# A decoder layer on one core: score and sum matmuls moved next to each other in TensorE's order

## The chip, the core and the metric

The kernel runs on one core of a Trainium2 chip. The metric is the device time of one execution in microseconds; less is better. The core's engines run their own instruction streams and wait for each other by semaphores: TensorE (PE in the profile, with its weight loads as PEld), VectorE (DVE), ScalarE (ACT), GpSimd (POOL), and SyncE, which here issues DMAs (SPq is its queue).

## What is computed

32 sequences of 128 tokens by 256 features go through one pre-normalised decoder layer in fp32. Cut to what matters:

```python
x = x + linear_attention(layernorm(x))      # 16 heads of 16: q, k = elu(.)+1; causal sums
x = x + cross_attention(layernorm(x), ctx)  # 16 heads of 16: softmax(q k^T / 4) v
x = x + ffn(layernorm(x))                   # 256 -> 1024 (gated) -> 1024 -> 1024 -> 256
# causal linear attention, per head:
num = einsum('bhsd,bhsde->bhse', q, cumsum(k[..., :, None] * v[..., None, :]))
out = num / (einsum('bhsd,bhsd->bhs', q, cumsum(k)) + 1e-6)
# ffn: ternary weights w with a scale s per output column
h = silu(tlin(h, w1)) * tlin(h, w2); h = gelu(tlin(h, h1)); h = gelu(tlin(h, h2)); out = tlin(h, w3)
```

The kernel computes the causal sums as masked scores: k q^T for each head, everything above the diagonal set to zero, times v with a column of ones beside it, whose sum is the denominator.

## The kernel before

**Work and tiling.** Attention goes by groups g = 0 to 15 of two sequences (b = 0, 1). The feed-forward part goes by turns f = 0 to 7 of 512 tokens, that is of two groups. A turn is the steps `gate` (L918), `hidden` (L933) and `w3` (L948): each step is a run of 4 matmuls of 128x128 weights by 512 columns. A turn of the feed-forward part has 16 gate steps, 64 hidden steps and 8 w3 steps, and the attention steps of later groups are strewn among them.

**Steps that use a part of the array.** The helper `scores` (L816) makes for one sequence the scores of 16 heads: contraction over 32 rows, four row quarters of the array at a time (`tile_position=(32 * r, 0)`), into four banks. It serves three steps: `lin_scores` (operands `qf,kz`), `max` (`xkz,xqf`; only to find the row maxima) and `x_scores` (`xqf,xkz`, behind four small bf16 matmuls at L809 that add the shift). The profile counts 32 matmul records for one such step. The helper `add_up` (L789) multiplies scores by values: outputs of 32 columns, four column quarters of the array (`tile_position=(0, 32 * j)`), 16 records for two tiles of scores (a "pair"). Its steps are `lin_sums` (`att_l,v`) and `x_sums` (`att_x,xv`), four pairs per group: pairs 0 and 1 for the first sequence, 2 and 3 for the second. All other matmuls and transposes use the whole array.

**What happens around them.** Linear attention: `lin_scores` b, then for each of its four tiles n `lin_copy` on ScalarE (L533, PSUM to `att_l`) and on GpSimd (L469, times the causal mask); `lin_sums` pair; `lin_out` on ScalarE (L500, PSUM to `sums`); `lin_turn` on TensorE (L798, transposes), then VectorE divides. Cross attention: `x_scores` b, `x_exp` on ScalarE (L563), `x_sums`, `x_out` (L500), `x_turn` (L798). `att_l` and `att_x` are rings of `NL, NX = 4, 4` tiles. `bias` on GpSimd (L475) adds a bias to the residual input `xb`. `load_ctx` on SyncE (L421) loads the context of the next group once its last readers on TensorE are through, for `xv` (L775) and `xk`; `ring` on SyncE (L388) loads the next weights into one of 4 slots once the matmuls that read the slot are through. ScalarE's gelu (L593, L599) releases the banks of `hidden`.

**What sets the order.** A table of numbers. `steady(name, n, engine=t, ...)` puts a step of group g into each named engine's list at nominal time begin(g) + stretch * t (2.2 from group 4 on), and `put` does so for the feed-forward steps. Each list is sorted by nominal time, and every engine executes its list in that order, blocking at a wait. The nominal time sets the order and nothing else. TensorE's list then goes through a planner that gives each step its PSUM bank(s), the ones that are nominally free first, and that puts a step back if none is free; `wait_pbank` makes the step wait for the last reader of that bank.

## Time and profile before

| | |
|---|---|
| time, median of 3 runs | 1188.05 us (1187.08 to 1190.3) |
| time of the profiled execution | 1188.87 us |
| its span in the profile | 1187.1 us |
| TensorE busy | 1139.9 us, 96% of the span |
| ScalarE, VectorE, GpSimd busy | 51%, 50%, 29% |
| chain that ended last, TensorE's share | 91% |

The span runs from the first to the last instruction; 1.8 us of the time lie outside it. The share of a busy TensorE counts a matmul from its start to its end, so a start that comes late behind another matmul's end is not seen as idle. The chain follows the end of the program back, instruction by instruction, to what released each.

### The profile page before, as it was taken

To read this page: it belongs to the slowest core of one execution; us is meant where nothing else is said; L and a number is where in the kernel's file an instruction comes from. 1 tells how busy PE (TensorE), PEld (TensorE's weight loads), DVE (VectorE), ACT (ScalarE), POOL (GpSimd) and SP (SyncE) were. 2 spreads that over 40 slices of the span, in tenths; PEclk is the share of its full clock that TensorE was granted. 3 is DMA by queue.
4 is the path that set the end of the run, shared out by engine and by line. 5 is a ranking of instruction groups with operands and counts; after the bars stand their busy time and mean duration, and the time that the engine had idled before them with its cause. 6 is when DMAs were issued, how large, how long until landed. Compare 5 with 4: busy or idle time off the path is not lost.

```text
span 1187.1 us, 24494 instructions
## 1 busy us (share of the span) xinstructions
PE 1139.9 (96%) x9666; PEld 902.2 (76%) x9666; DVE 588.0 (50%) x1381; ACT 601.3 (51%) x1078; POOL 339.8 (29%) x378
## 2 busy tenths in 40 slices
PE   4777999999999999999999999999999999999997
PEld 3665878778787877878777787877877787787886
DVE  2545653348344564535555465445744456443511
ACT  2345464635538365474645546374563736545432
POOL 3334260132503244042430415213250233400300
PEclk8899999999999999999999999999999999999999
DMA  3143554234423343325333253322442335333742
GB/s 112 63 151 91 152 187 160 90 110 157 144 76 108 133 161 121 97 93 175 109 122 105 81 182 120 128 94 92 170 144 84 106 127 169 106 106 116 245 149 73
DMA packets 62500, 148.58 MB, mean 125 GB/s; under 512 B 5936, under 2 KB 21424, under 8 KB 62384
## 3 DMA queue, kind: packets, MB, share of 16 engines
q1 hardware_dynamic: 58928, 135.44, 34.3%
q10 hardware_dynamic: 3456, 11.54, 3.2%
q8 instruction: 80, 1.31, 0.4%
q14 instruction: 36, 0.29, 0.1%
HBM read 130.17 MB, written 28.31 MB: 134 GB/s over the span
## 4 chain that ended last, share of the span: by engine, by line
PE 91%; DMA 3%; DVE 2%; issue 1%; ACT 1%; POOL 1%; SPq 0%; ACTq 0%; POOLq 0%; DVEq 0%
PE bank L933 41%; PE bank L918 10%; PE bank L766 9%; PE bank L816 8%; PE bank L789 5%; PE bank L775 5%; PE bank L948 5%; PE bank L798 2%; PE bank L758 2%; PE bank L874 2%; DMA ctxs<-in_ctxT 2%; PE bank L809 1%; DMA weight_ring<-weights_scratch 1%; POOL att_l L469 1%; PE bank L891 1%
## 5 line engine op out<-in xcount | busy, mean ns | idle before, releaser
L933 PE MATMUL bank<-hidden_b,weight_ring 128*128 128x512 f32 x1024 | 272.0, 407 | 0.0
L933 PE MATMUL bank<-hidden_a,weight_ring 128*128 128x512 f32 x1024 | 270.4, 406 | 0.0
L469 POOL TENSOR_TENSOR att_l<-att_l,cst 128x512 f32<-128x512 f32 x128 | 165.1, 1301 | 345.1 <-ACT att_l L533 344.7
L933 PEld LDWEIGHTS bank<-hidden_a,weight_ring 128*128 128x128 f32 x1024 | 185.4, 188 | 43.7 <-issue 6.9
L933 PEld LDWEIGHTS bank<-hidden_b,weight_ring 128*128 128x128 f32 x1024 | 184.2, 188 | 44.4 <-issue 6.7
L593 ACT ACTIVATE hidden_full<-bank,columns_sb 128x512 f32<-128x512 f32 x128 | 88.2, 689 | 197.9 <-PE bank L933 196.9
L918 PE MATMUL bank<-hidden_b,weight_ring 128*128 128x512 f32 x512 | 143.3, 414 | 0.7 <-DVE mx L689 0.6
L480 POOL TENSOR_TENSOR hidden_a<-hidden_full,hidden_a 128x512 fp32r<-128x512 f32 x64 | 82.2, 1290 | 171.7 <-ACT hidden_a L588 171.7
L629 DVE TENSOR_SCALAR denom<-bank 128x16 f32<-128x16 f32 x64 | 11.1, 174 | 203.6 <-PE bank L798 203.5
L918 PEld LDWEIGHTS bank<-hidden_b,weight_ring 128*128 128x128 f32 x512 | 91.7, 188 | 19.5 <-DVE mx L689 1.3
L728 DVE TENSOR_TENSOR hidden_b<-hidden_full,hidden_b 128x512 fp32r<-128x512 f32 x64 | 44.4, 695 | 116.9 <-ACT hidden_b L599 116.9
L451 POOL TENSOR_TENSOR ve<-mv,eps 128x1 f32<-128x1 f32 (+1 forms) x80 | 23.4, 292 | 256.3 <-DVE mv L608 256.3
L689 DVE TENSOR_REDUCE mx<-bank 128x4 f32<-128x512 f32 x128 | 83.8, 682 | 17.6 <-PE bank L816 17.6
L728 DVE TENSOR_TENSOR hidden_a<-hidden_full,hidden_a 128x512 fp32r<-128x512 f32 x64 | 44.4, 694 | 86.3 <-ACT hidden_a L599 86.0
L533 ACT ACTIVATE att_l<-bank 128x512 f32<-128x512 f32 x128 | 74.8, 606 | 18.1 <-PE bank L816 18.1
L563 ACT ACTIVATE att_x<-bank 128x512 f32<-128x512 f32 x128 | 66.4, 603 | 21.7 <-PE bank L816 21.6
L500 ACT ACTIVATE sums<-bank 128x256 f32<-128x256 f32 x128 | 47.2, 391 | 50.7 <-PE bank L789 50.3
L948 PE MATMUL bank<-hidden_a,weight_ring 128*128 128x512 f32 x256 | 68.0, 406 | 0.7 <-DMA weight_ring<-weights_scratch 0.7
L720 DVE SCALAR_TENSOR_TENSOR hidden_full<-hidden_full,bank 128x512 f32<-128x512 f32 x64 | 43.7, 683 | 29.2 <-ACT hidden_full L583 29.1
L583 ACT ACTIVATE hidden_full<-bank,s1h 128x512 f32<-128x512 f32 x64 | 44.0, 687 | 23.9 <-PE bank L918 21.1
L723 DVE SCALAR_TENSOR_TENSOR hidden_full<-bank,s,hidden_full 128x512 f32<-128x512 f32 x64 | 48.1, 751 | 14.1 <-PE bank L918 12.3
L948 PEld LDWEIGHTS bank<-hidden_a,weight_ring 128*128 128x128 f32 x256 | 46.9, 188 | 10.6 <-DMA weight_ring<-weights_scratch 1.5
(98 smaller groups left out, 1682.7 us busy)
## 6 DMA issues: line engine op xcount, KB each, us to landing
weight_ring<-weights_scratch SPq DMA_DIRECT2D x160, 512.0 KB, 3.4
weights_scratch<-in_h ACTq DMA_DIRECT2D x16, 512.0 KB, 4.5
xn3T_scratch<-hidden_b SPq DMA_DIRECT2D x16, 512.0 KB, 5.9
weight_ring<-weights_scratch SPq DMA_DIRECT2D x32, 256.0 KB, 2.9
weight_bits<-in_h SPq DMA_DIRECT2D x32, 256.0 KB, 3.7
x_in<-in_x SPq DMA_DIRECT2D x16, 256.0 KB, 4.0
xb<-in_x SPq DMA_DIRECT2D x16, 256.0 KB, 5.1
ctxs<-in_ctxT SPq DMA_DIRECT2D x16, 256.0 KB, 3.8
```

The costliest lines, as they stand in the source:

```text
L469: eng.tensor_tensor(slot, slot, causal.rearrange("p (o s) -> p o s", o=1).broadcast_to([P, 4, S]), ALU.mult)\
L480: eng.tensor_tensor(HA[:, 1, n, :], full[:, n % NFULL, :], HA[:, 0, n, :].bitcast(F32), ALU.subtract)\
L533: eng.activation(att_l[:, (NU * g + n) % NL, :, :], pbank("lin_scores", g, n)[:, :].rearrange("p (j s) -> p j s", j=4), ACT.Copy)\
L563: eng.activation(att_x[:, (NU * g + n) % NX, :, :], pbank("x_scores", g, n)[:, :].rearrange("p (j s) -> p j s", j=4), ACT.Exp, scale=SCALE ...
L593: eng.activation(full[:, (KH + n) % NFULL, :], pbank("hidden", g, n)[:, :], ACT.Gelu, scale=sc).then_inc(h_full, 1)
L689: eng.tensor_reduce(mx[:, b, 4 * r:4 * r + 4], pbank("max", g, n)[:, :].rearrange("p (j t) -> p j t", j=4), AX.X, ALU.max).then_inc(max_do ...
L728: eng.tensor_tensor(dst[:, 1, m, :], full[:, (KH + n) % NFULL, :], dst[:, 0, m, :].bitcast(F32), ALU.subtract)\
L766: mm = eng.matmul(pbank(step, g)[:, m * T:(m + 1) * T], w[:, c, m * P:(m + 1) * P], src[:, c, :], start=(c == 0), stop=(c == C - 1))
L816: mm = eng.matmul(pbank(step, g, 4 * b + r)[:, j * S:(j + 1) * S], stationary(rows, e, m, b), moving(rows, e, m, b), start=not shifted, st ...
L918: mm = eng.matmul(pbank(step, g, n)[:, :], ring[:, n // 4, at_:at_ + P], HB[:, part, kk, :], start=(kk == 0 and part == 0), stop=(kk == C ...
L933: mm = eng.matmul(pbank(step, g, n)[:, :], ring[:, slot, kk * P:(kk + 1) * P], src[:, part, kk, :], start=(kk == 0 and part == 0), stop=(k ...
L948: mm = eng.matmul(pbank(step, g, c)[:, :], ring[:, slot, kk % 4 * P:(kk % 4 + 1) * P], HA[:, part, kk, :], start=(kk == 0 and part == 0), ...
```

## The change

In the table the two pairs of one sequence get one nominal time (from group 4 on; earlier groups keep two), and a new pass goes over TensorE's sorted list: where of two steps among `lin_scores`, `max`, `x_scores`, `lin_sums`, `x_sums` only `gate`, `hidden` or `w3` steps stand between and the nominal times lie less than `JOIN = 1.59` apart, the earlier one is moved to stand directly in front of the later. Both pairs of a sequence now share one bank (`u = 2 * m + pair % 2`), which is waited for once and read by one ScalarE copy of 128x512 in place of two of 128x256. The rings `att_l` and `att_x` get 8 tiles. Some forty numbers of the table change besides, among them the places of `bias`, `lin_copy`, `load_ctx`, `ring` and of the tests of the weights' low bits (`load_bits`, `low_bits`). What the matmuls compute does not change.

```diff
@@ -34,6 +34,7 @@
     QUARTER = TURN / 88
     EARLY = ((0, 1.15), (28, 1), (66, 1.3), (110, 1.91))
     STRETCH = 2.2
+    JOIN = 1.59
...
-        steady("k", tensor=-5.41, scalar=-4.5, vector=-3.74)
+        steady("q", tensor=-8, scalar=-6.79, vector=-5.41)
+        steady("k", tensor=-4.93, scalar=-4.02, vector=-3.26)
...
+        steady("v", tensor=-4.17, vector=-0.29)
+        steady("load_xb", sync=0.96)
+        steady("bias", gpsimd=7.57)
+        steady("load_ctx", sync=8.45)
         for b in range(GB):
-            steady("lin_scores", b, tensor=-0.25 + 4.6 * b)
+            steady("lin_scores", b, tensor=-0.73 + 4.6 * b)
         for n in range(NU):
-            u = 0.32 + 1.35 * n
-            steady("lin_copy", n, scalar=u + 0.02, gpsimd=u - 1.61)
-            if n % 2:
-                steady("lin_sums", n // 2, tensor=u + 1.7)
-                steady("lin_out", n // 2, scalar=u + 2.98)
+            u = 0.32 + 1.07 * n
+            steady("lin_copy", n, scalar=u + 0.02, gpsimd=u - 0.41)
         for b in range(GB):
+            for h in range(2):
+                if early:
+                    u = 3.37 + 5.4 * b + 2.64 * h
+                else:
+                    u = 4.37 + 6.89 * b + 0.01 * h
+                steady("lin_sums", 2 * b + h, tensor=u + 0)
+            steady("lin_out", b, scalar=u + 0.41)
             u = 7.2 + 5.4 * b
-            steady("lin_turn", b, tensor=u - 0.33, vector=u - 0.03)
...
-            steady("project", b, tensor=u + 3.54, vector=u + 4.38, gpsimd=u + 3.93)
+            steady("project", b, tensor=u + 3.8, vector=u + 4.38, gpsimd=u + 5.74)
...
-            w = 30.6 + 3 * b + 0.15 * u
+            w = 30.6 + 3.62 * b + 0.15 * u
             steady("x_exp", n, scalar=w - 0.09)
-            if u % 2:
-                steady("x_sums", n // 2, tensor=w + 0.71)
-                steady("x_out", n // 2, scalar=w + 1.54)
         for b in range(GB):
+            for h in range(2):
+                if early:
+                    u = 31.75 + 3.07 * b + 0.3 * h
+                else:
+                    u = 31.42 + 3.72 * b + 0.01 * h
+                steady("x_sums", 2 * b + h, tensor=u - 0.1)
+            steady("x_out", b, scalar=u + 0.83)
             u = 27.6 + 3.21 * b
-            steady("shift", b, vector=u - 0.34, tensor=u + 0.29, scalar=u + 0.9)
+            steady("shift", b, vector=u - 0.87, tensor=u - 0.42, scalar=u + 0.9)
             u = 34.4 + 7.19 * b
-            steady("x_turn", b, tensor=u - 0.09, vector=u - 0.4, gpsimd=u + 0.29)
-            steady("ln3", b, vector=u + 3.82)
+            steady("x_turn", b, tensor=u - 1.47, vector=u - 0.36, gpsimd=u + 1.64)
+            steady("ln3", b, vector=u + 3.63)
 
 
...
             elif j < RING:
-                u = (-14.33, -1.3, -6.15, 0.27)[j]
+                u = (-8.49, -0.79, -6.15, 0.01)[j]
...
-            put(at, "ring", f, j, sync=u - 5.45)
+            put(at, "ring", f, j, sync=u + 0.35)
...
-            u = 193.16 + 110.03 * i + 18 * j
-            put(0, "load_bits", i, j, sync=u - 0.79)
-            put(0, "low_bits", i, j, vector=u + 14.31)
+            u = 185.4 + 116.28 * i + 18.39 * j
+            put(0, "load_bits", i, j, sync=u - 1.28)
+            put(0, "low_bits", i, j, vector=u + 11.62)
...
+    order = program["tensor"]
+    for i in reversed(range(len(order))):
+        if order[i][1] in ("lin_scores", "max", "x_scores", "lin_sums", "x_sums"):
+            j = i - 1
+            while j > 0 and order[j][1] in ("gate", "hidden", "w3"):
+                j -= 1
+            if j >= 0 and order[j][1] in ("lin_scores", "max", "x_scores", "lin_sums", "x_sums") and order[i][0] - order[j][0] < JOIN:
+                order.insert(i - 1, (order[i][0], *order.pop(j)[1:]))
...
-            NL, NX = 4, 4
+            NL, NX = 8, 8
...
-                    "lin_sums": ("scalar", "lin_out", sums_done[0], NU // 2), "x_sums": ("scalar", "x_out", sums_done[1], NU // 2),
+                    "lin_sums": ("scalar", "lin_out", sums_done[0], GB), "x_sums": ("scalar", "x_out", sums_done[1], GB),
...
                 t, step, g, n = pending.pop()
                 if step in ("hidden", "w3"):
                     uses = [n // 4] if n % 4 == 0 else []
+                elif step in ("lin_sums", "x_sums"):
+                    uses = [n // 2] if n % 2 == 0 else []
                 elif step in ("lin_scores", "max", "x_scores"):
...
-                def sums_out(which, step, g, pair):
-
-                    eng.wait_ge(summed[which], 4 * g + pair + 1)
-                    if pair % 2 == 0:
-                        wait_count(eng, sums_turned[which], GB * g + pair // 2)
-                    eng.activation(sums[:, which, :, :].rearrange("p (c q) s -> p q c s", q=2)[:, pair % 2],
-                                   pbank(step, g, pair)[:, 0:2 * S].rearrange("p (c s) -> p c s", c=C), ACT.Copy)\
+                def sums_out(which, step, g, b):
+
+                    eng.wait_ge(summed[which], 4 * g + 2 * b + 2)
+                    wait_count(eng, sums_turned[which], GB * g + b)
+                    eng.activation(sums[:, which, :, :], pbank(step, g, b)[:, :].rearrange("p (u s) -> p u s", u=4), ACT.Copy)\
                        .then_inc(sums_done[which], 1)
...
                     b = pair // 2
                     eng.wait_ge(ready, NU * g + 2 * pair + 2)
-                    wait_pbank(eng, step, g, pair)
+                    if pair % 2 == 0:
+                        wait_pbank(eng, step, g, b)
                     for m in range(C):
                         for n in (2 * pair, 2 * pair + 1):
                             for e in range(2):
                                 j = 2 * (n % 2) + e
-                                mm = eng.matmul(pbank(step, g, pair)[32 * j:32 * j + 32, m * S:(m + 1) * S],
+                                u = 2 * m + pair % 2
+                                mm = eng.matmul(pbank(step, g, b)[32 * j:32 * j + 32, u * S:(u + 1) * S],
                                                 vt[:, b, 8 * m + 2 * (n % 4) + e, :], att[:, (NU * g + n) % slots, 2 * m + e, :],
                                                 start=True, stop=True, tile_position=(0, 32 * j))
                     mm.then_inc(summed[which], 1)
 
                 def turn_sums(step, which, g, b):
-                    eng.wait_ge(sums_done[which], 4 * g + 2 * b + 2)
+                    eng.wait_ge(sums_done[which], GB * g + b + 1)
                     wait_pbank(eng, step, g, b)
```

**TensorE's order.** The first place is group 8's first sequence between the second cross-attention scores of group 7 (L809 and L816 `xqf,xkz`) and the sums of group 8, before:

```order
L809 MATMUL bank<-shiftT,onesb 128x512 x4
L816 MATMUL bank<-xqf,xkz 128x128 x16
L933 MATMUL bank<-hidden_b,weight_ring 128x512 x12
L798 MATMUL bank<-cst,sums 128x128 x4
L789 MATMUL bank<-att_x,xv 32x128 x8
L789 MATMUL bank<-att_l,v 32x128 x8
L789 MATMUL bank<-att_x,xv 32x128 x8
L933 MATMUL bank<-hidden_b,weight_ring 128x512 x4
L816 MATMUL bank<-qf,kz 128x128 x16
L933 MATMUL bank<-hidden_b,weight_ring 128x512 x12
L789 MATMUL bank<-att_l,v 32x128 x8
```

The same place of the changed kernel (its L812 is the sums, L839 the scores, L956 `hidden`):

```order
L832 MATMUL bank<-shiftT,onesb 128x512 x4
L839 MATMUL bank<-xqf,xkz 128x128 x16
L956 MATMUL bank<-hidden_b,weight_ring 128x512 x4
L821 MATMUL bank<-cst,sums 128x128 x4
L956 MATMUL bank<-hidden_b,weight_ring 128x512 x12
L839 MATMUL bank<-qf,kz 128x128 x16
L812 MATMUL bank<-att_x,xv 32x128 x16
L812 MATMUL bank<-att_l,v 32x128 x16
L956 MATMUL bank<-hidden_b,weight_ring 128x512 x16
```

The linear scores of the second sequence, both pairs of `x_sums` and both pairs of `lin_sums` now stand in one run; the second pair of `lin_sums` (last row before) has moved ahead of twelve `hidden` matmuls.

**SyncE's order.** The second place is the load of the context of group 5 (`ctxs`) among the weight loads, before:

```order
L388 DMA weight_ring<-weights_scratch 128x1024 x3
L397 DMA weight_bits<-in_h 128x512
L388 DMA weight_ring<-weights_scratch 128x1024
L421 DMA ctxs<-in_ctxT 128x2x256
L371 DMA x_in<-in_x 128x2x256
```

And of the changed kernel:

```order
L411 DMA weight_ring<-weights_scratch 128x1024
L420 DMA weight_bits<-in_h 128x512
L411 DMA weight_ring<-weights_scratch 128x1024 x2
L444 DMA ctxs<-in_ctxT 128x2x256
L394 DMA x_in<-in_x 128x2x256
```

The context load now goes out one weight load earlier: of the four weight loads that stood ahead of it here three are left.

**GpSimd's order.** The third place is the first group: the masks of its eight tiles (`att_l`) and the bias on `xb`, before:

```order
L469 TENSOR_TENSOR att_l<-att_l,cst 128x512 x6
L475 TENSOR_TENSOR xb<-xb,bob 128x512
L469 TENSOR_TENSOR att_l<-att_l,cst 128x512 x2
```

And of the changed kernel:

```order
L492 TENSOR_TENSOR att_l<-att_l,cst 128x512 x8
L498 TENSOR_TENSOR xb<-xb,bob 128x512
```

The bias has moved behind the last two masks; so it has in the later groups.

## Rows read from the trace of the kernel before

**Rows 1.** The page: span, and busy time of each engine.

```profile
span 1187.1 us, 24494 instructions
...
PE 1139.9 (96%) x9666; PEld 902.2 (76%) x9666; DVE 588.0 (50%) x1381; ACT 601.3 (51%) x1078; POOL 339.8 (29%) x378
```

**Rows 2.** Windows of the span: PE, PEld, DVE, ACT, POOL busy, PE clock, DMA.

```profile
0.00:121.50 121.50, 85.33 (x1033) 66.30 (x1034) 53.62 (x164) 46.41 (x99) 47.09 (x63) 0.92 0.33 102
...
545.70:687.10 141.40, 141.24 (x1210) 111.73 (x1209) 74.94 (x175) 76.78 (x136) 42.50 (x46) 1.00 0.36 122
...
1111.30:1187.10 75.80, 69.00 (x306) 56.75 (x304) 18.99 (x30) 24.49 (x39) 6.56 (x6) 0.99 0.39 128
```

**Rows 3.** Chain that ended last, 504 to 540: start us, us, what.

```profile
517.37 1.45 PE bank L789 x48
518.81 1.14 PE bank L933 x4
...
524.02 0.57 PE bank L789 x16
...
538.83 0.92 PE bank L933 x4
```

**Rows 4.** TensorE's timeline, 61 to 63.6: start us, us, instruction.

```profile
61.23 1.07 PE L816 MATMUL bank<-xqf,xkz 32*128 32x128 f32 x32
62.23 0.65 PE L789 MATMUL bank<-att_l,v 128*32 128x128 f32 x16
```

**Rows 5.** TensorE's timeline, 504 to 520.

```profile
505.04 1.06 PE L816 MATMUL bank<-xqf,xkz 32*128 32x128 f32 x32
506.03 2.11 PE L933 MATMUL bank<-hidden_b,weight_ring 128*128 128x512 f32 x8
...
512.67 0.39 PE L809 MATMUL bank<-shiftT,onesb 2*128 2x512 bf16 x4
```

**Rows 6.** All engines' waits: engine, line, waited for: us, times, longest.

```profile
PE bank L775 <- DMA ctxs<-in_ctxT: 2.1, 3, 1.2
```

**Rows 7.** The queues' timeline (SyncE), 303 to 320.

```profile
307.23 7.47 SPq L388 DMA_DIRECT2D weight_ring<-weights_scratch  x3
...
319.10 0.32 SPq L388 DMA_DIRECT2D weight_ring<-weights_scratch  x1
319.52 0.38 SPq L421 DMA_DIRECT2D ctxs<-in_ctxT  x1
```

**Rows 8.** The chain, 318 to 332.

```profile
319.52 5.57 DMA ctxs<-in_ctxT
...
325.13 1.99 PE bank L775 x8
```

**Rows 9.** The chain, 27 to 36 and 107 to 120.

```profile
30.70 1.23 POOL xb L475
...
34.43 1.08 PE bank L789 x16
...
113.33 1.23 POOL xb L475
```

**Rows 10.** ScalarE's groups: line, operation, shapes, count, busy, mean ns.

```profile
L533 ACT ACTIVATE att_l<-bank 128x512 f32<-128x512 f32 x128 | 74.8, 606 | 18.1 <-PE bank L816 18.1
...
L500 ACT ACTIVATE sums<-bank 128x256 f32<-128x256 f32 x128 | 47.2, 391 | 50.7 <-PE bank L789 50.3
```

**Rows 11.** ScalarE's timeline, 504 to 521.

```profile
510.14 0.68 ACT L599 ACTIVATE hidden_a<-bank,columns_sb 128x512 fp32r<-128x512 f32 x1
...
514.15 2.07 ACT L563 ACTIVATE att_x<-bank 128x512 f32<-128x512 f32 x4
...
519.44 0.61 ACT L533 ACTIVATE att_l<-bank 128x512 f32<-128x512 f32 x1
```

**Rows 12.** GpSimd's timeline, 510 to 526.

```profile
520.12 1.39 POOL L469 TENSOR_TENSOR att_l<-att_l,cst 128x512 f32<-128x512 f32 x1 [2.07 <-ACT att_l L533]
```

More of the change, by code:

```diff
@@ L48, in decoder_layer_program @@
         at, stretch = begin(g)
+        early = g < len(EARLY)
         def steady(step, n=0, **slots):
             put(at, step, g, n, stretch, **slots)
-        steady("load_x", sync=-21.29)
-        steady("ln1_stats", vector=-14.57, gpsimd=-14.11)
-        steady("ln1", vector=-10.72)
+        steady("load_x", sync=-21.65)
+        steady("ln1_stats", vector=-18.26, gpsimd=-16.9)
+        steady("ln1", vector=-11.07)
         steady("ln1T", tensor=-9.02, scalar=-8.85)
-        steady("q", tensor=-8.4, scalar=-6.79, vector=-5.28)
@@ L58, in decoder_layer_program @@
-        steady("k", tensor=-5.41, scalar=-4.5, vector=-3.74)
+        steady("q", tensor=-8, scalar=-6.79, vector=-5.41)
+        steady("k", tensor=-4.93, scalar=-4.02, vector=-3.26)
         steady("k_heads", vector=-3.21)
-        steady("v", tensor=-4.49, vector=-1.75)
-        steady("load_xb", sync=1.83)
-        steady("bias", gpsimd=6.19)
-        steady("load_ctx", sync=9.29)
+        steady("v", tensor=-4.17, vector=-0.29)
+        steady("load_xb", sync=0.96)
+        steady("bias", gpsimd=7.57)
@@ L73, in decoder_layer_program @@
+        for b in range(GB):
+            for h in range(2):
[5 more added lines that the diff above has]
+            steady("lin_out", b, scalar=u + 0.41)
             u = 7.2 + 5.4 * b
-            steady("lin_turn", b, tensor=u - 0.33, vector=u - 0.03)
+            steady("lin_turn", b, tensor=u - 0.33, vector=u + 0.45)
             steady("o_turn", b, tensor=u + 1.41, scalar=u + 2)
-            steady("project", b, tensor=u + 3.54, vector=u + 4.38, gpsimd=u + 3.93)
@@ L77, in decoder_layer_program @@
-            steady("ln2", b, vector=u + 6.1)
-        steady("ln2T", tensor=18.75, scalar=19.89)
-        steady("xq", tensor=20.91, scalar=22.32)
-        steady("xk", tensor=16.95, scalar=17.71)
-        steady("xv", tensor=12.26, scalar=18.48)
+            steady("project", b, tensor=u + 3.8, vector=u + 4.38, gpsimd=u + 5.74)
+            steady("ln2", b, vector=u + 6.15)
+        steady("ln2T", tensor=18.94, scalar=19.14)
+        steady("xq", tensor=20.91, scalar=22.03)
+        steady("xk", tensor=16.95, scalar=21.19)
@@ L82, in decoder_layer_program @@
+        steady("xv", tensor=12.26, scalar=17.81)
         for b in range(GB):
@@ L119, in decoder_layer_program @@
         for p in range(2):
-            put(at, "xn3T", 2 * f + p, tensor=-10.32 + 2.6 * p, scalar=-8.56 + 2.6 * p, vector=-7.36 + 2.6 * p)
+            put(at, "xn3T", 2 * f + p, tensor=-9.46 + 2.6 * p, scalar=-5.61 + 2.6 * p, vector=-6.5 + 2.6 * p)
             put(at, "x2T", 2 * f + p, tensor=10.79 + 1.5 * p, scalar=12.21 + 1.5 * p)
-        put(at, "keep_xn", f, sync=5.63)
-        put(at, "keep_x2", f, sync=19.84)
+        put(at, "keep_xn", f, sync=10.53)
+        put(at, "keep_x2", f, sync=15.41)
         for m in range(KH):
@@ L129, in decoder_layer_program @@
             put(at, "gated", f, m, vector=u + 2 * QUARTER + 0.54)
-            put(at, "gate_round", f, m, scalar=u + 2 * QUARTER + 5.26)
-            put(at, "gate_rest", f, m, gpsimd=u + 2 * QUARTER + 3.78)
+            put(at, "gate_round", f, m, scalar=u + 2 * QUARTER + 5.16)
+            put(at, "gate_rest", f, m, gpsimd=u + 2 * QUARTER + 4.74)
         for n in range(2 * KH):
@@ L147, in decoder_layer_program @@
             if f == 0 and j < RING:
-                u = -32.71 + j
+                u = -33.84 + j
             elif j < RING:
-                u = (-14.33, -1.3, -6.15, 0.27)[j]
+                u = (-8.49, -0.79, -6.15, 0.01)[j]
             elif j < 2 * RING:
```

## Prediction

> **What bounds the kernel now.** I read the page first: TensorE is busy for 1139.9 of 1187.1 us, ScalarE for 51%, VectorE for 50%, GpSimd for 29% [rows 1]. The windows show where the rest lies: in the first 121.5 us TensorE works for 85.33, after that it is as good as never idle (141.24 of 141.40 us in one turn of the feed-forward part, the last 75.8 us apart) [rows 2]. So between 121.5 and about 1111 us whatever shortens TensorE's stream shortens the kernel, and whatever shortens another engine's does nothing. Busy is not the same as useful, though, and for that the chain of the end is the view, since it gives to each run of matmuls the time by which it holds up the next. Four `hidden` matmuls cost 0.92 us behind a whole-array step, and 1.14 behind sums, though they are the same instructions [rows 3]. One pair of sums by itself costs 0.57, three pairs in a run 1.45 [rows 3]: a further pair costs (1.45 - 0.57) / 2 = 0.44, the first 0.13 more. So a run of steps on quarters of the array pays 0.13 us to begin (if it begins with sums) and 0.21 to end (1.13 less 0.92). The change takes away such beginnings and ends.
>
> **Fewer runs.** I counted the runs in the two orders of TensorE: 169 before, 116 after. From group 3 on, a group had eleven (two `max`, two `x_scores`, two `lin_scores`, five of sums) and has seven. Up to the first `gate` step there are 17 and 16, so nearly the whole saving, 52 runs, falls where TensorE bounds. At 0.21 each that is 52 x 0.21 = 10.9 us. Places at which sums begin (behind the whole array or behind scores) are 85 before and 61 after, 15 and 16 of them up to the first `gate`, so 70 and 45 in the part that counts: 25 x 0.13 = 3.25 us. That scores to sums costs the same 0.13 as whole array to sums is the one price that has to be argued, since there are 27 such places (scores, then sums) where there were 4, and 10 the other way where there were 4. One of the four shows scores starting at 61.23 and the sums behind them at 62.23, 1.00 apart; scores with `hidden` behind them have 505.04 and 506.03, 0.99 apart [rows 4, 5]. Going from row quarters to column quarters holds the array up just as going to the whole array does, so it isn't free. It could be cheaper at the other end only if nothing were paid in the run's first sums: then I lose nothing of the sum and gain 29 x 0.13 = 3.8 us. It could cost an end and a beginning, 0.34: then 29 x 0.21 = 6.1 us go back. I take 0.13, by the row. Sum: 10.9 + 3.25 = 14.2 us.
>
> The Trainium skill, in TensorEngine Tiling (Array Packing), section Tiling Modes, says that changing the tiling mode, not just the tile, drains TensorE. By that rule scores next to sums save only one of two drains, and only sums next to sums, or scores next to scores, save both. The trace agrees, with its 1.00 and 0.99 us; with a free change the sum would be the 3.8 us larger.
>
> **Context loads.** TensorE waits three times, 2.1 us in all, for the context that `xv` reads [rows 6]. One of them: the load goes out at 319.52, takes 5.57 us, and `xv` starts at 325.13 [rows 7, 8]. It goes out then because the weight load ahead of it in SyncE's queue waited until 319.10 for its slot [rows 7]. Now the load stands in front of that weight load, behind one that had gone out by 307.23 + 7.47 = 314.70 [rows 7]. That is over 4 us earlier against a longest wait of 1.2, so I take the whole of it: 2.1 us. The weight load itself has three other slots' worth of matmuls as cover.
>
> **The first 121.5 us.** Here chains of all engines bound, and the bias on GpSimd is in them twice, 1.23 us each, between masks that the last sums of a sequence wait for [rows 9]. It now follows the masks: -2.5 us, unless at the first place other work of ScalarE takes over (the sums started at 34.43 [rows 9]). Against this each exposed copy of a sequence's sums is one of 128x512 where the last of two of 128x256 was waited for. ScalarE takes 606 ns for a 128x512 copy and 391 for a 128x256 one [rows 10]: 0.2 us more, at some five places on the chain, +1.0. Together 1.5 us. The order of a dozen other steps changes here too, and TensorE's clock is at its lower level for part of this stretch (mean 0.92 [rows 2]), so this term may be 2.5 us off either way.
>
> **New waits where TensorE bounds.** A wait that recurs in each of 13 groups costs 13 times itself, so I looked at three, around 512 us.
> (1) The second `lin_sums` pair moves ahead of twelve matmuls. It needs mask 3, which ended at 520.12 + 1.39 = 521.51, as its ScalarE copy ran only at 519.44 [rows 11, 12]. By the chain's prices the pair now stands at about 520.6: second `x_scores` at 512.5 (512.67 less one end), 1.2 for it, four `hidden` 1.1, `x_turn` 0.4, twelve `hidden` 2.8, scores 1.1, two `x_sums` pairs 1.0, one `lin_sums` pair 0.4. Unmoved, the mask would cost 0.9. But the copy is now put right behind the four exponentials, which end at 514.15 + 2.07 = 516.22 [rows 11] and may come half a microsecond later: copy to about 517.4, mask to 518.8. 1.8 us to spare.
> (2) The second `x_scores` needs the bank of the first `x_sums`, now freed by one copy. Before it on ScalarE stand the gelu that ends at 510.14 + 0.68 = 510.82 [rows 11] and two 128x512 copies; copies follow each other at 0.5 us, so the bank is free at 510.82 + 3 x 0.5 + 0.1 = 512.4. TensorE gets there at 512.5 [rows 5]. Nothing to spare: between 0 and 0.5 us in the six or so groups that lie like this.
> (3) Eight tiles in each ring take away the waits of ScalarE's copies for sums; that only helps.
> I put 1.0 us for all of this, with 0 and 4 as its ends.
>
> **Sum.** 14.2 + 2.1 + 1.5 - 1.0 = 16.8 us off the profiled 1188.9: 1172.1. The median of the runs is 0.8 us below that execution, so 1171.3; I say 1171.5. With the terms' ends (changes of mode 3.8 less or 6.1 more, start-up 2.5, waits 1 and 3) this case reaches from 1166 to 1178; chance 0.72.
>
> **Rivals.**
> *Change of mode dear.* Scores to sums costs an end and a beginning: 6.1 us more, 1177.5. Against it stand the 1.00 and 0.99 us; for it, that the end of a run on the whole array is paid partly in its first matmuls, which these two starts don't show. Chance 0.08.
> *Packed runs starve.* Three microseconds of scores and sums in one run fill banks faster than ScalarE, at 606 ns a bank [rows 10], reads them, and (1) or (2) turns into 0.4 to 0.9 us in each of 13 groups: 5 to 12 us back, 1176.5 to 1183.5. For it: no slack at (2), and 0.9 us at (1) if the copy slips. Against: ScalarE is idle for half of its time. Chance 0.10.
> The page just named says, under PSUM Bottleneck, that tiling speeds up TensorE but not the reading of its results, which may become the limit; that speaks for this rival, and the 606 ns are its measure here.
> *Slower.* In ScalarE's queue the copy of the linear sums stands ahead of the next gelu and waits for the whole run of scores and sums; if the gelu comes late, its bank and then `hidden` do. The run ends at about 521.0, the copies of the sums by 522.3, and the gelu's matmuls end at about the same time, so I see no delay. It decides from 16.8 / 13 = 1.3 us a group on: with 2 us a group, 26 in all, it would be 1171.5 + 26 = 1197.5. Chance 0.04.
> *No change.* The runs get fewer but TensorE was waiting on something else under cover of long matmuls. About 1188. The prices 0.21 and 0.13 come from a stretch in which TensorE doesn't wait, so I give this 0.03.
> *More.* A change of mode half paid, and start-up shorter by 4: 1163 to 1166. Chance 0.03.
>
> **How the numbers follow.** The predicted time is that of the first case. The range 1163.5 to 1181 holds it, the dear change, two thirds of the starving case and most of the last: about 0.88 by these chances; I keep it so because the start-up is ordered anew in more places than I could price. Repeated runs differ by 0.3%, 3.6 us; faster than 1184.5 are all cases but the last two signs, slower and no change: 0.93. Within 0.3% 0.03, slower 0.04.
>
> **What would show it.** In the changed kernel's chain: sums behind scores in one piece with a single 1.1 us `hidden` group behind them; sums of two pairs 0.88 to 1.0; a turn of the feed-forward part (141.4 us now) at about 139.2, since two groups save 2.2; no wait for `ctxs`; no `xb` on the chain before the first gate. It is wrong if a turn takes 140 or more, or if waits of sums for `att_l` or of scores for `sums` recur with each group.

## The result, and the profile of the changed kernel

The changed kernel takes 1172.53 us (median of 4 runs, 1168.11 to 1174.07) where the kernel before takes 1188.68 (1187.08 to 1190.3) beside it: ratio 0.9858, 95% interval 0.9827 to 0.9889. Its profiled execution took 1171.52 us, with a span of 1169.7. The prediction was 1171.5.

The page of the changed kernel, to be held against [rows 1]:

```profile
span 1169.7 us, 24358 instructions
...
PE 1127.3 (96%) x9666; PEld 907.8 (78%) x9666; DVE 600.8 (51%) x1381; ACT 593.3 (51%) x1014; POOL 341.8 (29%) x378
```

The same number of matmuls keeps TensorE busy for 12.6 us less, and ScalarE issues 64 instructions less (64 copies of sums in place of 128). The windows, now for the stretch up to the first `gate`, one turn, and the end (to be held against [rows 2]):

```profile
0.00:117.30 117.30, 86.00 (x1028) 67.12 (x1029) 53.33 (x161) 45.43 (x89) 47.18 (x63) 0.88 0.33 105
545.50:684.50 139.00, 138.76 (x1209) 112.34 (x1208) 75.53 (x175) 75.69 (x129) 42.96 (x46) 1.00 0.37 122
1100.00:1169.70 69.70, 63.21 (x281) 51.92 (x279) 14.50 (x25) 20.70 (x33) 1.29 (x1) 0.99 0.36 122
```

The start-up has got shorter although its mean clock is lower, 0.88: up to the first `gate` TensorE ran 27.3 us at its lower clock, in the profile of the kernel before 20.5. The turn takes 139.0 us with as many matmuls as the 141.4 of before. From the starts of the `gate` batches in both traces: up to the first 119.82 and 116.97 us (-2.85); first to second 147.08 and 144.35 (-2.73); second to seventh, five turns or ten groups, 708.85 and 698.57 (-10.28); seventh to eighth -1.38; from there to the end -0.16. Together the 17.4 us by which the spans differ.

The chain of the end, around the place that the prediction looked at (start us, us, what):

```profile
500.38 1.10 PE bank L839 x32
501.48 1.01 PE bank L812 x32
502.49 2.04 PE bank L956 x8
...
510.07 1.10 PE bank L839 x32
511.17 1.88 PE bank L812 x64
513.05 1.16 PE bank L956 x4
...
516.23 1.44 DVE weight_bits L759
...
518.29 0.67 DVE xn L632
...
519.36 0.43 DVE o L657
...
519.84 0.44 PE bank L889 x2
```

L839 is the helper of the scores here, L812 that of the sums, L956 `hidden`, L889 `o_turn`. The upper rows show what was meant to happen: scores, then two or four pairs of sums (1.01 and 1.88 us) in one piece, and one slow group of `hidden` (1.16) behind it. The lower rows show what nobody had asked for: the chain leaves TensorE and goes through VectorE, whose test of the weights' low bits and whose normalization `xn` (step `ln3`) stand ahead of the division `o` that `o_turn` waits for. TensorE's waits say how often (us, times, longest):

```profile
PE bank L889 <- DVE o L657: 7.0, 12, 1.3
```

Before, the same wait was 3.6 us in 4 places. A wait for `ctxs` is no longer among TensorE's.

To see where ten groups' time goes I took, for each change from one kind of matmul to another in the five turns, the time from the last start of the one to the second start of the other, and called a wait what it exceeded the usual time of that kind by (usual over all the kernels of this document). Before: 704.45 us of regular stream and 4.4 of waits (2.85 of them three waits for `ctxs`). After: 693.05 and 5.5 (4.65 of them `o_turn`). So the regular stream gave 11.40 us in ten groups, and the waits took 1.1 back.

### The profile page after: what moved, and what is told of

It is laid out like the page before. It is cut to its first block, busy times and chain, and to the rows that moved or that the text cites. A ratio compares the mean times of both kernels' runs of the same rounds, so it can differ in the third digit from the quotient of the medians.

```text
span 1169.7 us, 24358 instructions
## 1 busy us (share of the span) xinstructions
PE 1127.3 (96%) x9666; PEld 907.8 (78%) x9666; DVE 600.8 (51%) x1381; ACT 593.3 (51%) x1014; POOL 341.8 (29%) x378
## 4 chain that ended last, share of the span: by engine, by line
PE 89%; DVE 4%; ACT 3%; issue 2%; POOL 1%; DMA 0%; SPq 0%; ACTq 0%; POOLq 0%; DVEq 0%
PE bank L956 37%; PE bank L941 10%; PE bank L787 9%; PE bank L839 8%; PE bank L971 5%; PE bank L796 5%; PE bank L812 5%; PE bank L897 3%; PE bank L779 2%; PE bank L821 2%; DVE xn L632 1%; PE bank L832 1%; PE bank L889 1%; ACT L614 1%; PE bank L914 1%
## 5 line engine op out<-in xcount | busy, mean ns | idle before, releaser
L956 PE MATMUL bank<-hidden_b,weight_ring 128*128 128x512 f32 x1024 | 264.7, 403 | 0.0
L956 PE MATMUL bank<-hidden_a,weight_ring 128*128 128x512 f32 x1024 | 264.0, 403 | 0.0
L956 PEld LDWEIGHTS bank<-hidden_a,weight_ring 128*128 128x128 f32 x1024 | 186.0, 188 | 40.7 <-issue 4.4
L956 PEld LDWEIGHTS bank<-hidden_b,weight_ring 128*128 128x128 f32 x1024 | 184.9, 188 | 41.3 <-issue 3.8
L941 PE MATMUL bank<-hidden_b,weight_ring 128*128 128x512 f32 x512 | 140.4, 411 | 0.0
L971 PE MATMUL bank<-hidden_a,weight_ring 128*128 128x512 f32 x256 | 67.8, 406 | 0.0
L522 ACT ACTIVATE sums<-bank 128x512 f32<-128x512 f32 x64 | 37.3, 603 | 41.2 <-PE bank L812 41.2
```

What stands on the lines that cost most here:

```text
L941: mm = eng.matmul(pbank(step, g, n)[:, :], ring[:, n // 4, at_:at_ + P], HB[:, part, kk, :], start=(kk == 0 and part == 0), stop=(kk == C ...
L956: mm = eng.matmul(pbank(step, g, n)[:, :], ring[:, slot, kk * P:(kk + 1) * P], src[:, part, kk, :], start=(kk == 0 and part == 0), stop=(k ...
L971: mm = eng.matmul(pbank(step, g, c)[:, :], ring[:, slot, kk % 4 * P:(kk % 4 + 1) * P], HA[:, part, kk, :], start=(kk == 0 and part == 0), ...
```

## Experiments

Times are medians; the kernel before stood at 1189.12, 1188.61 and 1189.46 us in the three sets.

**1. The pairs apart again.** The changed kernel with no joining pass and, for every group, the numbers of the early ones, so that pairs and scores stand alone again (167 runs on quarters of the array; 116 in the changed kernel). One bank for both pairs, the rings and all other numbers stay.

```diff
-    JOIN = 1.59
+    JOIN = 0
...
-                    u = 4.37 + 6.89 * b + 0.01 * h
+                    u = 3.37 + 5.4 * b + 2.64 * h
...
-                    u = 31.42 + 3.72 * b + 0.01 * h
+                    u = 31.75 + 3.07 * b + 0.3 * h
```

> The changed kernel with the two pairs of a sequence apart again in the table (the numbers of the early groups for all) and without the pass that joins; one bank, 8 tiles and all other new numbers stay. 167 runs in TensorE's order instead of 116, and sums begin at 98 places instead of 61. Theory (switching is paid for by TensorE): 51 x 0.21 + 37 x 0.13 = 15.5 us slower than the changed kernel, so about 1187 to 1188 us. Rival (the other numbers of the table made the gain): within 4 us of the changed kernel, 1170 to 1176.

1187.17 us, ratio 0.9989 (0.9978 to 1.0): nearly the whole gain is gone. The five turns take 712.30 us, 13.7 more than in the changed kernel: 705.48 of regular stream, 12.4 more, and 6.8 of waits, 1.3 more, now mostly of `lin_turn` for the sums' copy (the line below counts the whole execution). In these ten groups the edit makes 40 more runs and 30 more places at which sums begin, by the prices 40 x 0.21 + 30 x 0.13 = 12.3 us. It is not quite the order of before, in which sums begin at 85 places and not at 98, and its five turns are 3.45 us longer than those of before. A shorter start-up (first `gate` at 113.0 us) hides this in the time.

```profile
PE bank L821 <- ACT sums L522: 6.0, 9, 1.0
```

**2. The pass alone taken away.** `JOIN = 0`, nothing else: 119 runs.

> The changed kernel with JOIN = 0: the pass moves nothing. The table alone already puts most of these steps side by side: 119 runs instead of 116. Theory: 3 x 0.21 + 0.13 = 0.8 us slower than the changed kernel, not to be told from it (1171 to 1175). Rival (the pass is what joins): 10 us or more slower.

1171.52 us, 0.9855 (0.9833 to 0.9878), and five turns of 698.52 us. The pass moves next to nothing; the numbers of the table had put the steps side by side.

**3. The core on the old table.** The kernel before with the pass, the new places of the sums, one bank and rings of 8 tiles, and everything else of its table as it was: 132 runs.

```diff
-            if n % 2:
-                steady("lin_sums", n // 2, tensor=u + 1.7)
-                steady("lin_out", n // 2, scalar=u + 2.98)
+            for h in range(2):
+                if early:
+                    u = 3.37 + 5.4 * b + 2.64 * h
+                else:
+                    u = 4.37 + 6.89 * b + 0.01 * h
+                steady("lin_sums", 2 * b + h, tensor=u + 0)
+            steady("lin_out", b, scalar=u + 0.41)
...
-            NL, NX = 4, 4
+            NL, NX = 8, 8
```

> The kernel before with only the core of the change: sums of a sequence at one time, one bank, one copy, 8 tiles, the joining pass; all other numbers of the table as before. 132 runs instead of 169, sums begin at 74 places instead of 85. Theory by prices alone: 37 x 0.21 + 11 x 0.13 = 9.2 us faster than before, 1179.5. Rival (the steps around it must move too): the second pair of linear sums now comes before its mask, which ended at 521.5 where the pair stands at 520.6, and waits 0.9 us or more in each of 13 groups, 12 us back: 1188 to 1192, with waits of sums for att_l in the trace.

1181.95 us, 0.9949 (0.9932 to 0.9965). 7.2 us faster than before, where the prices gave 9.2. Fewer runs saved (regular stream 697.85, 6.6 less than before), and the sums wait for masks:

```profile
PE bank L812 <- POOL att_l L492: 3.8, 7, 1.8
```

Of these 3.8 us, 2.5 are two places of the start-up, where the kernel before waits too (2.0 us in 2 places). What recurs is 0.27 us in one group of each of five turns, at the place that the prediction called (1):

```profile
517.74 0.65 PE L812 MATMUL bank<-att_l,v 128*32 128x128 f32 x16 [0.27 <-POOL att_l L492]
```

The changed kernel has no such wait, so other numbers of the table keep it away; that it is those of `lin_copy` was not tested by itself. The recurring wait is 1.35 us in all, far from the 12 of the rival. The two profiled executions differ by 8.4 us: 3.0 of them in the five turns, 3.0 between the first and the second `gate` batch, 1.7 in the start-up.

**4. What a switch costs between row and column quarters.** The changed kernel with one pair of `x_sums` put ahead of the `lin_scores` it followed, in 11 groups. The lengths of all runs stay. Each of the 11 now begins with sums in place of scores and has one change from sums to scores more; the changes from scores to sums stay 27. (The trace has 72 places at which sums begin, 45 + 27; the 79 in the expectation is a slip.)

```diff
+    for i in range(len(order) - 2):
+        if order[i][2] >= 3 and order[i][1] == "lin_scores" and order[i + 1][1] == order[i + 2][1] == "x_sums":
+            order[i], order[i + 1] = (order[i][0], *order[i + 1][1:]), (order[i + 1][0], *order[i][1:])
```

> The changed kernel with one pair of x_sums moved in front of the linear scores of the second sequence, inside the same run, in 11 groups: same number of runs and of places at which sums begin behind the whole array or scores (79 instead of 61 by kind: 45 behind the whole array, 27 behind scores, and 21 instead of 10 places at which scores follow sums). Theory (a change between row and column quarters costs one drain, 0.13): 11 x 0.13 = 1.4 us slower than the changed kernel in TensorE's stream, and scores start 0.20 us after the last matmul of the sums. Rival (an end and a beginning, 0.34): 3.7 us slower, and 0.35 or more between them.

1175.13 us, 0.989 (0.9869 to 0.9911). The regular stream grows by 1.0 us in ten groups, about 0.1 for each added change, against 1.3 (10 x 0.13) by the theory and 3.4 by the rival. `o_turn` waits 2.4 us more, and the five turns take 3.4 us more; the medians differ by 2.6. TensorE's timeline of this kernel (its lines are 3 further down: L815 sums, L842 scores):

```profile
511.30 0.65 PE L815 MATMUL bank<-att_x,xv 128*32 128x128 f32 x16
511.87 1.17 PE L842 MATMUL bank<-qf,kz 32*128 32x128 f32 x32
512.98 0.64 PE L815 MATMUL bank<-att_x,xv 128*32 128x128 f32 x16
513.43 1.06 PE L815 MATMUL bank<-att_l,v 128*32 128x128 f32 x32
```

A pair takes 0.57 from its start to the start of scores, and 0.45 to the start of another pair: this change costs some 0.12, not the 0.34 of the dear rival. The last matmul start before a change and the first behind it lie 0.20 us apart in both directions; from pair to pair it is 0.09.

**5. Rings of 4 tiles.** The changed kernel with `NL, NX = 4, 4`.

> The changed kernel with rings of 4 tiles instead of 8 for att_l and att_x. Theory (the rings are no bound once sums come in one run): within 3 us of the changed kernel, 1172 to 1175. Rival (the room is what lets copies and masks run ahead of the joined sums): copies of tiles 4 to 7 wait for sums, ScalarE's queue blocks behind them, and 0.4 us or more per group come back, 1178 or more.

1178.16 us, 0.9923 (0.9904 to 0.9941): 5.6 us slower than the changed kernel by the medians, and the five turns alone take 7.4 us more (705.96). ScalarE's timeline:

```profile
447.17 0.60 ACT L554 ACTIVATE att_l<-bank 128x512 f32<-128x512 f32 x1 [4.38 <-PE bank L812]
447.78 1.28 ACT L614 ACT_TABLE_LOAD   x1
449.08 0.69 ACT L614 ACTIVATE hidden_full<-bank,columns_sb 128x512 f32<-128x512 f32 x1
...
450.23 1.08 ACT L522 ACTIVATE sums<-bank 128x512 f32<-128x512 f32 x2
```

The fifth copy of scores needs a tile that the sums, now late and together, still have to read. ScalarE stands for 4.38 us in front of it, and the gelu and the copies of sums behind it are late, so `o_turn`'s waits grow to 16.0 us in 12 places (12.1 in the five turns). I had put the larger rings down as something that "only helps". Without them over a third of the gain is lost by the medians, and over half by the traces, where the stretch from the second `gate` batch to the eighth is 8.9 us longer; the medians come from executions at different clocks (this kernel four of six at 0.991, the changed one two of four at 0.986).

**6. The context load on the kernel before.** Only the numbers of `load_ctx` and `ring` from the change.

```diff
-        steady("load_ctx", sync=9.29)
+        steady("load_ctx", sync=8.45)
...
-                u = (-14.33, -1.3, -6.15, 0.27)[j]
+                u = (-8.49, -0.79, -6.15, 0.01)[j]
...
-            put(at, "ring", f, j, sync=u - 5.45)
+            put(at, "ring", f, j, sync=u + 0.35)
```

> The kernel before with only SyncE's new places for the context load and the weight loads. Theory: the waits of xv for ctxs (2.1 us in 3 places) are gone, 2 us faster than before: 1186 to 1187. Rival (the load is hidden or comes no earlier): waits and time as before.

1185.73 us, 0.9978 (0.9966 to 0.999), 2.9 us faster. The five turns take 705.34 us in place of 708.85. Of these 3.5 us the waits for `ctxs` are 2.85; a `w3` matmul that started 0.57 us late behind a weight load is on time too, by the new places of `ring`. In the changed kernel SyncE's queue reads (start us, us, issue), against [rows 7]:

```profile
304.75 4.44 SPq L411 DMA_DIRECT2D weight_ring<-weights_scratch  x2
309.29 0.38 SPq L444 DMA_DIRECT2D ctxs<-in_ctxT  x1
```

**7. The bias.** Once on the kernel before (`bias` from 6.19 to 8.3, behind the masks), once on the changed kernel, back to its old place (7.57 to 6.19).

> The kernel before with only the bias on GpSimd moved behind the masks. Theory: the two places of 1.23 us on the chain before the first gate step go, the first gate starts 1.5 to 2.5 us earlier (119.8 us from the start before), and the time falls by as much, 1186.5. Rival: another engine takes over there, first gate within 0.5 us of before.

1189.66 us, 1.0009 (0.9998 to 1.002): nothing. The chain goes through `xb` as it did in [rows 9], only behind the last mask, and VectorE's addition of the projection, which reads it, is next:

```profile
116.62 1.26 POOL att_l L469
117.88 1.24 POOL xb L475
119.21 0.43 DVE x L678
```

> The changed kernel with the bias (xb) back at its old number in GpSimd's order, ahead of the last masks of a group. Theory, after before_bias: the place of the bias moves the start-up by less than 1 us, and in the steady groups it puts 1.2 us of GpSimd ahead of two of the eight masks, which PE now reads a little later than before, so nothing or a few waits of lin_sums for att_l: 1172 to 1174. Rival, the start-up term of the prediction: the bias ahead of the masks lengthens the start-up by some 2.5 us and the time is 1174.5 to 1176, with the first gate batch 2 us later than the 117.3 of the changed kernel.

1170.57 us, 0.984 (0.9827 to 0.9853), not distinguishable from the changed kernel by the medians. But here the executions of one kernel have to be read with their mean clock. The changed kernel took 1173.53 and 1174.07 us at 0.986, and 1168.11 at 0.992. The one with the old bias took 1174.98 at 0.986, 1170.87 at 0.992, and 1168.96 to 1170.57 at 0.993. At like clocks it is 1 to 3 us slower, though that rests on five executions. Its first `gate` comes at 120.2 us, with 30.7 us at the lower clock; in the kernel of experiment 5, which has the bias behind the masks, and rings of 4 besides, it comes at 118.8 with the same 30.7. Its chain before the first `gate` says where 1.23 of them are:

```profile
111.10 2.56 POOL att_l L492 x2
113.66 1.23 POOL xb L498
114.89 2.46 POOL att_l L492 x2
...
117.40 0.64 PE bank L812 x16
```

In the changed kernel no `xb` is on this chain: its four last masks follow each other, the bias ends at 115.08, and the addition waits 0.32 us for it. With the bias moved on the kernel before, the last mask first waits 1.09 us for its copy on ScalarE, the bias starts at 117.84, and the addition waits 2.44 us. In the five turns the bias changes nothing (698.53 against 698.57).

**8. The new wait.** Three kernels, all with the changed one as their base. `turn_early` gives the divisions of `lin_turn` on VectorE their old number. `ln3_late` puts `ln3` of a group's first sequence behind the next group's first division. `best` does both.

```diff
-            steady("lin_turn", b, tensor=u - 0.33, vector=u + 0.45)
+            steady("lin_turn", b, tensor=u - 0.33, vector=u - 0.03)
...
-            steady("ln3", b, vector=u + 3.63)
+            steady("ln3", b, vector=u + 4.5 - 0.87 * b)
```

(In `best` the second line reads `u + 4.2 - 0.57 * b`, which puts it behind that division as well.)

> The changed kernel with VectorE's division of the linear sums at its old place (vector = u - 0.03 instead of u + 0.45). In the changed kernel the transposes of o wait 12 times, 7.0 us in all, for this division, before 4 times and 3.6 us. Theory (the new place, behind ln3 and the test of the low bits, makes the waits): these waits fall to about 4 us, 2 to 3 us faster than the changed kernel, 1169.5 to 1170.5. Rival (TensorE is simply earlier, and the division is late wherever it stands): same waits, same time.

> The changed kernel with ln3's normalization of a group's first sequence 0.87 later, behind the next group's first division, and nothing else. Theory: the waits of o_turn at the first sequence (some 0.45 us in each turn) go, those behind the low_bits tests stay: 2 to 3 us faster than the changed kernel, 1169.5 to 1170.5. Together with turn_early and best it shows whether the two moves add. Rival: the wait was for something else that ends at the same time (the second sequence's sums or the tensor_reduce), and the time stays within 1 us of the changed kernel's 1172.5.

> The changed kernel with two entries of VectorE's order moved: lin_turn's divisions 0.48 earlier (as in turn_early), and ln3's normalization of a group's first sequence 0.57 later, which puts it behind the next group's first division instead of ahead of it. Theory: the wait of the o_turn transposes (L889) for VectorE's division is what the change added, 0.44 to 0.45 us in each turn at the first sequence, because ln3's xn (0.67 us, 1.39 us where GpSimd runs masks beside it) stands ahead of the division. In turn_early 3.1 us of it are left in the ten groups between the second and the last gate batch; here nearly all of them go, some 3 to 4 us in 16 groups: 1163.5 to 1165 us where turn_early is 1167.5. Rival: the normalization, now late, holds up what stands behind it (the gelu_rest whose hidden tile is next, or xn3T's transposes), and the time is no better than turn_early, 1167 to 1170, with new waits of PE for xn or hidden tiles.

| | us | ratio (95%) | five turns, us | `o_turn` waits in them |
|---|---|---|---|---|
| changed kernel | 1172.53 | 0.9858 (0.9827 to 0.9889) | 698.57 | 4.65 |
| turn_early | 1167.53 | 0.9831 (0.9814 to 0.9848) | 696.99 | 3.1 |
| ln3_late | 1163.15 | 0.979 (0.9769 to 0.9811) | 694.38 | 0.5 |
| best | 1164.7 | 0.9797 (0.9782 to 0.9812) | 694.13 | 0.25 |

By the traces `turn_early` is worth less than its median: 1.6 us in the five turns, and all of it at one place (380 us), where a test of the low bits stood ahead of the division. At the five places of 0.45 us `ln3` stands directly ahead of the division in both, and in the kernel before. Of the 4.0 us between the two profiled executions 2.7 are the start-up, which both order alike, with 17.1 us at the lower clock in place of 27.3. So the theory holds for a part of the waits and the rival, that the division is late wherever it stands, for the rest.

Why these five wait is to be seen in the changed kernel at 448 us, on VectorE, on GpSimd and on TensorE:

```profile
448.35 1.39 DVE L632 TENSOR_SCALAR xn<-x,mv,rstd 128x256 f32<-128x256 f32 x1
449.66 0.16 DVE L650 TENSOR_SCALAR denom<-bank 128x16 f32<-128x16 f32 x1
...
450.14 0.42 DVE L657 TENSOR_TENSOR o<-bank,rec 128x256 f32<-128x256 f32 x1
```

```profile
448.27 4.38 POOL L492 TENSOR_TENSOR att_l<-att_l,cst 128x512 f32<-128x512 f32 x3 [3.15 <-ACT att_l L554]
```

```profile
447.95 0.60 PE L821 MATMUL bank<-cst,sums 128*128 128x128 f32 x4
448.30 2.08 PE L956 MATMUL bank<-hidden_a,weight_ring 128*128 128x512 f32 x8
450.62 0.44 PE L889 MATMUL bank<-cst,o 128*128 128x128 f32 x2 [0.24 <-DVE o L657]
```

The division had its operand ready and stood behind a normalization that nothing needed yet, and that took 1.39 us here. In the kernel before the same normalization was ahead of the same division and took as long, but the transposes came later:

```profile
454.55 1.38 DVE L611 TENSOR_SCALAR xn<-x,mv,rstd 128x256 f32<-128x256 f32 x1
456.63 0.17 DVE L629 TENSOR_SCALAR denom<-bank 128x16 f32<-128x16 f32 x1 [0.70 <-PE bank L798]
```

There VectorE waited 0.70 us for the transposes, which started at 455.99, 1.44 us behind the normalization. In the changed kernel they start at 447.95, 0.40 us ahead of it. So the change moved TensorE's transposes against the normalization, and the old order of VectorE no longer fitted. With `ln3_late` the order at a place of this kind is:

```profile
512.37 0.16 DVE L650 TENSOR_SCALAR denom<-bank 128x16 f32<-128x16 f32 x1
...
512.86 0.42 DVE L657 TENSOR_TENSOR o<-bank,rec 128x256 f32<-128x256 f32 x1
513.20 1.08 DVE L632 TENSOR_SCALAR xn<-x,mv,rstd 128x256 f32<-128x256 f32 x1
```

My expectation for `ln3_late` (2 to 3 us) was too small: it is 9 us faster than the changed kernel's median, the five turns give 4.2 of it. It also removes the waits behind the low-bit tests, which I had thought would stay, and so `best` has nothing to add; the two moves overlap. The other half is not the wait's but the clock's: in the profiled executions, which order everything up to there alike, the first `gate` comes at 113.3 us in place of 116.97, with 13.7 us at the lower clock up to it in place of 27.3. At like clocks (0.992) `ln3_late` took 1163.15 and 1163.69 us and the changed kernel 1168.11, some 4.5 to 5 us apart, which is what the trace accounts for. `best` and `ln3_late`, which the medians don't tell apart, beat both kernels: 2.0 to 2.1% less than before.

## Why the prediction came out right, and what in it was wrong

**The total: right partly by luck.** The prediction of 1171.5 us is 1.0 us off the median, and its terms are further off than that. The gains came out larger than forecast and the one loss four times as large, and this cancels. The clock alone moves the changed kernel's executions by 5.7 us.

**Fewer runs: right in mechanism, place and size.** The prices 0.21 and 0.13, read from one piece of the chain, gave 1.09 us a group; the five turns gave 1.14. (The row for the end of a run gives 1.14 less 0.92, that is 0.22; with it the ten groups, 40 runs and 20 beginnings of sums fewer, come to 11.4 us, as measured.) Experiment 1 puts the runs back and keeps the rest of the table, and the regular stream grows by 12.4 us where the same prices give 12.3. The disputed price, scores to sums, came out as argued: 0.20 us from the last start of scores to the first of sums in 23 places of the changed kernel, as from sums to scores in experiment 4. The ten groups have 20 such changes where there were none, so the dear rival gives 6.8 us for them (20 x 0.21 less than 11.0) and the free one 13.6, and both are out.

**Context loads: right, too small.** 2.1 us were the waits that the view lists; the start of the next matmuls behind such a wait is late too, which makes 2.85 in the five turns. Experiment 6 measures 2.9 us in time and 3.5 in the five turns, with the 0.57 us behind a weight load that the prediction had no term for.

**The first 121.5 us: the mechanism was half wrong.** I took 1.23 us twice off the chain because the bias left the masks. On the kernel before, moving it gave nothing (experiment 7); in the changed kernel it gives one 1.23, because there the masks' copies come in time and the bias behind them is still early enough for its reader. The step that failed is that a piece taken off the chain shortens it by its length: `xb` has a reader of its own, the projection's addition, which I did not follow. The term of 1.5 us was also too small, and the 2.85 us of the two traces hide by how much, since the changed kernel ran 6.8 us longer at the lower clock. Six other kernels here have the changed one's rings and its order of everything up to the first `gate`: with 13.7 us at the lower clock three of them reach it at 113.0 to 113.3 us, with 17.1 one (`turn_early`) at 114.3, and with 27.3 the changed kernel and two more (experiments 2 and 4) at 117.0 to 117.2. An estimate from these is about 115.1 with the 20.5 us of the kernel before, 4.7 us earlier than its 119.8 and beyond the 4.0 that the prediction allowed. One 1.23 of this is the bias; the kernel with experiment 6's edit has its first `gate` 2.1 us earlier than before, with 3.4 us less at the lower clock. Which of the reordered steps bring the rest was not tested.

**New waits: wrong places.** I had priced 1.0 us for masks and for the bank of `x_scores`. Neither waits in the changed kernel. Experiment 3 shows that on the old table the mask does, 0.27 us a turn. What came instead was a wait on VectorE that I had not looked at: the division stands behind `ln3`, as it did before, but TensorE's transposes now come before that normalization has run. The step that failed is the choice of the three waits to look at, all of them of ScalarE's and GpSimd's work and none of VectorE's. In ten groups the wait costs 4.65 us. The division's new number makes 1.6 of it (`turn_early`), and moving `ln3` alone takes away all but 0.5; the waits other than for `ctxs` grew from 1.55 to 5.5: 4.0 where 1.0 stood. I had named recurring waits of sums and scores as what would make the prediction wrong, and did not ask the same of the transposes between them. That the time still came out is luck: the error was hidden by the terms that were too small, context and start-up above all.

**The rivals.** Packed runs that starve: at 8 tiles not seen, at 4 tiles it is there (experiment 5) by another door, ScalarE's copy that stands in front of its gelu. That is also the mechanism of the slower rival; with a tile free it never came to that. The signs held for the most part: three of the five turns take 139.05 us against 139.2, and there is no wait for `ctxs` and no `xb` on the chain. But one turn takes 139.9 and one 141.5, over the 140 that I had named as a sign of being wrong: they hold the waits of 0.84 and 1.55 us behind the low-bit tests, and the 141.5 two others, of 0.5 and 0.35.

## What to carry to other kernels

When matmuls of different array shapes are strewn through a long stream, price the seams, not the matmuls: read in the chain what the same group costs behind each kind, count the seams in both orders, and multiply. Packing steps together makes their inputs pile up, so the buffers ahead of them have to grow with the run. After a reordering, list every wait of the busy engine, and look at what stands ahead of the released operation in the other engine's queue: here one cheap operation out of place cost over a quarter of what the change brought. To take a piece off the chain, follow its own reader first.

## What was not expected of the hardware

The normalization `xn` (128x256, VectorE) takes 0.38 us at the least, 0.41 in the median of its 64 places in the changed kernel, and up to 1.43. Sixteen of the 64 take longer than 0.42 us (0.67 to 1.43), and all of them start while a GpSimd operation is running, or within 0.003 us of its start, and end 0.15 to 0.16 us after its end, as at 448.35: the mask that began at 448.27 ended at 449.58, the normalization at 449.73. In the kernel before it is 15 of 64, with the same 0.15 to 0.16. The Trainium skill, in SBUF — State Buffer, section Terms, says that VectorE and GpSimd take a pair of SBUF ports in turn, each for a whole instruction, while the other stands still. The rows agree with it: the end of the normalization is tied to the end of the mask, and not to a share of its length. That it comes 0.15 us behind it, where the whole normalization takes 0.38 us alone, leaves open how much of it runs before. No experiment moved a mask for its own sake.

Changing between row quarters and column quarters leaves the same 0.20 us between the last start and the next either way. From sums to scores that is a cost of 0.12 us (experiment 4), about what it costs to go from the whole array to sums (0.13), and about half of what it costs to go back to the whole array (0.21).

The share of the start-up at the lower TensorE clock, 1.2 GHz, differs from execution to execution: from 13.7 to 30.7 us up to the first `gate` in the profiled ones, and kernels that order everything up to it alike had from 13.7 (experiment 1, first `gate` at 113.0 us) to 27.3 (the changed kernel, 117.0). In the changed kernel 0.006 of mean clock goes with 5.7 us of time (1168.11 us at 0.992, 1173.53 and 1174.07 at 0.986), so a median of five executions can be off by more than the effect of a small edit.
